# A transformer layer on one core: the ranks of the expert choice through memory instead of TensorE

## The chip, the cores and the metric

The kernel runs on one core of one Trainium2 chip. Its engines are TensorE (PE, with its weight loads PEld), VectorE (DVE), ScalarE (ACT), GpSimd (POOL) and SyncE (SP), which issues nearly all DMAs here. The metric is the device time of one execution in microseconds. Times of three runs and one profiled execution are given.

## What is computed

The input is x of shape (4, 1024, 128), all in fp32. The layer is a causal attention with 16 heads of 8, and then a layer of 8 experts of which each token uses one:

```python
x = x + attention(layernorm(x), Wq, bq, Wk, bk, Wv, bv, Wo, bo)      # causal softmax, 16 heads of 8
h = layernorm(x)
logits = h @ gate_w.T                                                # 8 experts
sel, rw = argmax(logits), sigmoid(max(logits))
for e in range(8):
    xs = h * (rw * (sel == e))[:, None]
    out = out + (xs @ w_up[e].T) * silu(xs @ w_gate[e].T) @ w_down[e].T    # inner size 64
x = x + out
```

## The kernel before, in words

The attention takes the first four fifths of the time: 16 units of 4 heads, each with its scores, exponentials and values. Behind it stand the **expert steps**, STEPS = 8, one for each half (512 tokens) of each of the 4 sequences. Each engine has a program of its own, written by hand in the order in which it runs, and semaphores between them; there is no scheduler.

Step n of the experts handles 512 tokens as 4 tiles of 128. The experts go in PAIRS = 4 pairs of 2 x 64 = 128 inner rows. TensorE computes for each pair a gate product into two banks in turn (`gate`, L1244) and an up product (`up`, L1249), both 128 x 512 in fp32, and each such call shows in the trace as two matmuls. ScalarE takes the silu of the gate (`back`, L808). VectorE multiplies by 1 or 0, depending on whether the token's expert is the one of the row (`choose`, L991), and by the up product (`back`, L997), which gives `hidden`. TensorE multiplies by the down weights (`down`, L1258), first pairs 0 and 1, then 2 and 3. VectorE adds the residual (`finish`, L1003, tile y), and SyncE stores y (`store`, L488).

`choose` must know for every token, along the free dimension and in all partitions, which expert it has. That is the **rank**: `residual(n)` on VectorE computes it with one token per partition, four numbers in each (`rank`, L974), at the end of the work of step n - 2. To get it into all partitions, TensorE multiplies, with each of the four columns broadcast as weights, by the identity (`spread_rank`, L1231) into a PSUM bank, and ScalarE copies the bank into `rank_b` (`copy_rank`, L789). In TensorE's order `spread_rank(n + 1)` stands between the two halves of `down(n)`, ahead of `turn_xs` (L1037), which transposes the scaled input `xs` of step n + 1; ScalarE's copy `copy_xs` (L793) takes that one into `xs_t`. VectorE prepares `xs` with `weigh_rows` (L979, L982).

Further back in the chain of a step stand the projection of the attention (`project3`, L1220) for step n + 2, in the middle of step n, and ahead of it GpSimd's product with the inverse sums (L658), which needs two DMAs: the reload of the attention values and of the inverses (`load_attn`, L459 and L461). SyncE's queue in the expert steps is: reload of step n, store of step n - 3, reload of step n + 1, and so on, each behind a semaphore wait. A wait there holds up all that is behind it. `invert` (L927) on VectorE and `store_inverse` (L454) give the inverses of the last batch early in step 2.

## Time and profile before

| what | us |
|---|---|
| median of 3 runs | 525.75 (525.52 to 526.53) |
| profiled execution | 523.49 |
| its span | 521.8 |
| one expert step (steps 2 to 6) | 12.03 |
| PE busy | 493.5 |
| DVE busy | 441.8 |
| ACT busy | 376.4 |
| POOL busy | 225.7 |

The span is the time between the first and the last instruction that the profiler has; what lies around it belongs to the execution too. Busy times of PE contain overlaps, since matmuls are pipelined. A profile names an instruction by its engine, the line of the kernel, the operation and the tiles out<-in. In a timeline a piece begins at the start of its first instruction, and a bracket behind it tells how long the engine sat idle before it and who released it. In the chain of waits each piece begins where the one before ends. The expert steps begin at 424.12 us of the span, and step 3, from which most rows below are, at 448.41.

### The profile page before, as it was taken

What the parts mean: (1) busy time and instruction counts of PE and PEld (TensorE: products, weight loads), DVE (VectorE), ACT (ScalarE), POOL (GpSimd) and SP (SyncE); (2) the same over time, 40 slices, a digit from 0 to 9 for tenths busy, and PEclk for the clock granted to TensorE, in tenths of its full rate; (3) what the DMA queues carried; (4) which work ended last, traced back from release to release, by engine and by line L of the source; (5) the groups of instructions that cost most, each with busy time, mean ns of one, the idle gap of its engine ahead of it and who ended that gap; (6) DMA issues with size and microseconds to landing.
All of it is one profiled execution on the core that took longest, in us unless ns stands there. A gap on an engine that the chain in (4) does not pass through costs nothing.

```text
span 521.8 us, 12773 instructions
## 1 busy us (share of the span) xinstructions
PE 493.5 (95%) x4797; PEld 218.2 (42%) x4797; DVE 441.8 (85%) x695; ACT 376.4 (72%) x790; POOL 225.7 (43%) x526
## 2 busy tenths in 40 slices
PE   7699799999999999999999999999999899999997
PEld 6565324333332433324333332433333236777764
DVE  6958799999999999999998999999995428888864
ACT  7254698888989888898888989888797872222321
POOL 5397266353453635446363444634344142222210
PEclk9889999999999999999999999999999999999999
DMA  6252023422203232221423202112030212221001
GB/s 176 58 137 62 12 74 80 103 62 76 74 19 96 69 92 63 28 71 30 107 60 78 74 10 68 40 53 69 13 94 19 61 39 67 61 63 62 20 22 40
DMA packets 33550, 32.63 MB, mean 63 GB/s; under 512 B 10448, under 2 KB 26960, under 8 KB 33488
## 3 DMA queue, kind: packets, MB, share of 16 engines
q1 hardware_dynamic: 33376, 31.48, 22.8%
q8 instruction: 38, 0.62, 0.5%
q10 hardware_dynamic: 112, 0.33, 0.2%
q14 instruction: 24, 0.20, 0.1%
HBM read 20.26 MB, written 11.01 MB: 60 GB/s over the span
## 4 chain that ended last, share of the span: by engine, by line
PE 59%; DVE 30%; POOL 3%; ACT 3%; issue 3%; DMA 1%; ACTq 0%; DVEq 0%; POOLq 0%
PE ps L1191 18%; DVE top_p L890 11%; PE ps L1175 10%; PE ps L1136 8%; DVE top_p L885 7%; DVE top_p L887 6%; PE ps L1258 5%; PE ps L1244 5%; PE ps L1249 5%; POOL xn L564 2%; ACT sum_sb L759 2%; PE ps L1220 2%; DVE top L906 2%; PE ps L1144 2%; ACT prob L768 1%
## 5 line engine op out<-in xcount | busy, mean ns | idle before, releaser
L768 ACT ACTIVATE prob<-ps 128x512 f32<-128x512 f32 (+2 forms) x640 | 303.9, 564 | 35.1 <-PE ps L1175 33.6
L645 POOL TENSOR_SCALAR_AFFINE_SELECT prob<-prob 128x256 f32<-128x256 f32 x256 | 99.8, 417 | 181.4 <-ACT prob L768 178.6
L1175 PE MATMUL ps<-q_rows,k_rows 51*128 51x512 bf16 (+3 forms) x768 | 170.8, 328 | 3.3 <-ACT prob L768 1.6
L1191 PE MATMUL ps<-prob,v_all 128*9 128x512 f32 (+3 forms) x1536 | 156.9, 488 | 2.3 <-POOL prob L645 0.7
L885 DVE TENSOR_REDUCE top_p<-ps 128x2 f32<-128x1024 f32 x128 | 150.9, 1220 | 9.6 <-PE ps L1136 8.6
L1136 PE MATMUL ps<-k_rows,q_rows 48*128 48x128 bf16 (+3 forms) x1024 | 113.3, 265 | 7.4 <-DVE top_p L890 4.5
L1175 PEld LDWEIGHTS ps<-q_rows,k_rows 51*128 51x128 bf16 x768 | 53.0, 94 | 148.2 <-ACT prob L768 131.3
L890 DVE TENSOR_REDUCE top_p<-ps 128x8 f32<-128x1024 f32 x64 | 76.6, 1220 | 10.7 <-PE ps L1144 10.2
L887 DVE TENSOR_REDUCE top_p<-ps 128x4 f32<-128x1024 f32 x64 | 75.2, 1215 | 1.8 <-PE ps L1136 1.8
L1136 PEld LDWEIGHTS ps<-k_rows,q_rows 48*128 48x128 bf16 x1024 | 45.4, 94 | 27.2 <-DVE top_p L890 9.0
L1191 PEld LDWEIGHTS ps<-prob,v_all 128*9 128x9 f32 x1536 | 24.3, 88 | 52.2 <-issue 29.5
L808 ACT ACTIVATE prob<-ps 128x512 f32<-128x512 f32 x32 | 19.1, 597 | 32.7 <-PE ps L1244 20.1
L991 DVE SCALAR_TENSOR_TENSOR prob<-rank_b,rank_of,prob 128x512 f32<-128x512 f32 x32 | 23.3, 750 | 16.1 <-ACT prob L808 15.3
L1244 PE MATMUL ps<-xs_t,w_g 128*128 128x512 f32 x64 | 31.6, 596 | 0.0
L1249 PE MATMUL ps<-xs_t,w_u 128*128 128x512 f32 x64 | 31.4, 592 | 0.0
L1258 PE MATMUL ps<-w_d,prob 128*128 128x128 f32 x256 | 31.0, 275 | 0.0
L1258 PEld LDWEIGHTS ps<-w_d,prob 128*128 128x128 f32 x256 | 29.9, 192 | 1.0 <-issue 1.0
L1144 PE MATMUL ps<-shade,pick 64*128 64x256 bf16 (+1 forms) x160 | 29.4, 296 | 0.0
L759 ACT ACTIVATE sum_sb<-ps 128x512 f32<-128x512 f32 x32 | 19.0, 594 | 13.4 <-PE ps L1191 13.4
L663 POOL TENSOR_SCALAR spread<-moments 128x4 f32<-128x4 f32 x8 | 1.6, 195 | 55.4 <-DVE moments L969 55.3
L892 DVE TENSOR_REDUCE top_p<-ps 128x16 f32<-128x1024 f32 x16 | 19.5, 1221 | 6.8 <-PE ps L1144 6.4
L789 ACT ACTIVATE rank_b<-ps 128x512 f32<-128x512 f32 x8 | 4.8, 600 | 27.5 <-PE ps L1231 27.5
(110 smaller groups left out, 451.8 us busy)
## 6 DMA issues: line engine op xcount, KB each, us to landing
split_parts<-part SPq DMA_DIRECT2D x12, 384.0 KB, 4.4
q_rows<-split_parts SPq DMA_DIRECT2D x31, 96.0 KB
k_rows<-split_parts SPq DMA_DIRECT2D x31, 96.0 KB
value_sums<-sum_sb SPq DMA_DIRECT2D x128, 18.0 KB
x_sb<-x SPq DMA_DIRECT2D x8, 256.0 KB, 4.2
qk<-value_sums SPq DMA_DIRECT2D x8, 256.0 KB, 3.6
qk<-inverse_sums SPq DMA_DIRECT2D x8, 256.0 KB, 4.0
out<-y SPq DMA_DIRECT2D x8, 256.0 KB, 2.3
```

The source lines that it names most:

```text
L645: last = g.affine_select(out=quarter, in_=quarter, pattern=[[0, GH], [1, Q]], base=Q * (1 - z), channel_multiplier=-1, compare_op=ALU.is_g ...
L768: a.activation(prob[:, i % NB, g0:g0 + heads, 0:cols], ps[:, load_at(u, n) % 3, 0:heads * cols].rearrange("p (s t) -> p s t", s=heads), AC ...
L885: return v.tensor_reduce(top_p[:, c, place, s:s + 3:2, m], banks, AX.X, ALU.max)
L887: return v.tensor_reduce(top_p[:, c, place, :, m], banks.rearrange("p r (s t) -> p (r s) t", s=2), AX.X, ALU.max)
L890: return v.tensor_reduce(top_p[:, c, place, :, :].rearrange("p g m -> p (g m)"), banks.rearrange("p r (y t) -> p (r y) t", t=P), AX.X, ALU ...
L1136: last = mm(ps[:, first_bank + rg, cols], q_rows[rows, k, c, s, q0:q0 + P], k_rows[rows, k, 0 if width == HALF else c, s, k0:k0 + width], ...
L1144: last = mm(dst, pick[rows, PICK[tile]:PICK[tile] + P], shade[rows, None, :].to_broadcast((64, len(blocks), Q)), start=False, stop=True, s ...
L1175: last = mm(ps[:, l % 3, m * cols:(m + 1) * cols], k_rows[rows, k, j // TPH, s + m, j % TPH * P:(j % TPH + 1) * P], q_rows[rows, k, c, s + ...
L1191: last = mm(ps[32 * g:32 * g + HD + 1, BANK_V, q0:q0 + n], v_all[:, b, j, first_head + g, :], prob[:, i % NB, g, 0:n], start=(j == 0), sto ...
L1244: mm(ps[:, BANK_GATE[pr % 2], :], w_g[:, pr * P:(pr + 1) * P], xs_t[:, h, :], start=True, stop=True).then_inc(gate_mm, 1)
L1249: mm(ps[:, BANK_UP[pr % 2], :], w_u[:, pr * P:(pr + 1) * P], xs_t[:, h, :], start=True, stop=True).then_inc(up_mm, 1)
L1258: last = mm(ps[:, BANK_DOWN, i * P:(i + 1) * P], hidden[:, pr, i * P:(i + 1) * P], w_d[:, pr, :], start=(pr == 0 and i == 0), stop=(pr == ...
```

## The change

From step 2 on, the rank no longer goes over TensorE, a bank and ScalarE. `rank` becomes fp32. SyncE writes its 512 numbers to a small tensor in memory (`ranks`), waits until they have landed, and reads them back as one row repeated into all 128 partitions of `rank_b` (`send_rank`). `choose` waits for that read. Step 1 keeps the old way, with a tile `rank_1` in bf16; TensorE's wait for its copy moves from the first gate product to the up product that uses its bank.

```diff
+    ranks = nc.dram_tensor("ranks", (STEPS, TPH, P), FP32, kind="Internal").ap()
...
-        rank = sb("rank", [P, 2, TPH], BF16)
+        rank_1 = sb("rank_1", [P, TPH], BF16)
+        rank = sb("rank", [P, 2, TPH])
...
+            def send_rank(n):
+                h = (n - 1) % 2
+                sp.wait_ge(rank_set, n)
+                sp.dma_start(ranks[n - 1].rearrange("i (p o) -> p i o", o=1), rank[:, h, :, None],
+                             allow_slow_non_contiguous=True).then_inc(rank_out, 16)
+                sp.wait_ge(rank_out, 16 * (n - 1))
+
+                hold(sp, chosen_set, 4 * (n - 2))
+                sp.dma_start(rank_b[:, h, :], ranks[n - 1:n].rearrange("o i p -> o (i p)").to_broadcast((P, HALF))
+                             ).then_inc(rank_in, 16)
...
             load_sums(BATCH - 1)
+            send_rank(2)
             store(0, 0)
+            send_rank(3)
...
                 reload(n)
                 store(*divmod(n - 4, 2))
-            for n in range(STEPS - 2, STEPS + 1):
+                send_rank(n - 1)
+            store(*divmod(STEPS - 3, 2))
+            send_rank(STEPS)
+            for n in range(STEPS - 1, STEPS + 1):
                 store(*divmod(n - 1, 2))
...
                 if more:
-                    copy_rank(n + 1, 1 - h)
                     copy_xs(n + 1, 1 - h)
...
-                v.tensor_reduce(rank[:, h, :], hit[:, h], AX.X, ALU.max).then_inc(rank_set, 1)
+                v.tensor_reduce(rank[:, h, :] if n > 1 else rank_1[:], hit[:, h], AX.X, ALU.max).then_inc(rank_set, 1)
...
-                dve.wait_ge(rank_b_set, n)
+                if n == 1:
+                    dve.wait_ge(rank_b_set, 1)
+                else:
+                    dve.wait_ge(rank_in, 16 * (n - 1))
...
             def gate(n, n4, h, pr):
                 if pr == 0:
-                    pe.wait_ge(rank_b_set, n)
                     pe.wait_ge(xs_t_set, n)
...
             def up(n4, h, pr):
                 hold(pe, hidden_set, n4 + pr - 1)
+                if (n4, pr) == (0, 1):
+
+                    pe.wait_ge(rank_b_set, 1)
...
                 down(n, n4, (0, 1))
                 if more:
-                    spread_rank(n + 1, 1 - h)
                     turn_xs(n + 1, 1 - h)
                 down(n, n4, (2, 3))
```

On TensorE, from the up products at the end of step 6 to the first gate products of step 7, before:

```order
L1249 MATMUL ps<-xs_t,w_u 128x512 [waits hidden_set] x2
L1220 MATMUL ps<-w_o,rest 128x136 [waits attn_set]
L1220 MATMUL ps<-w_o,rest 128x136 x3
L1258 MATMUL ps<-w_d,prob 128x128 [waits hidden_set,y_set]
L1258 MATMUL ps<-w_d,prob 128x128 x7
L1231 MATMUL ps<-ident_b,rank 128x128 [waits silu_set,rank_set]
L1231 MATMUL ps<-ident_b,rank 128x128 x3
L1037 MATMUL ps<-ident,xs 128x128 [waits xs_set]
L1037 MATMUL ps<-ident,xs 128x128 x3
L1258 MATMUL ps<-w_d,prob 128x128 [waits hidden_set]
L1258 MATMUL ps<-w_d,prob 128x128 x7
L1244 MATMUL ps<-xs_t,w_g 128x512 [waits silu_set,xs_t_set,rank_b_set]
```

And the same place after, where the lines of the file have other numbers (L1271 is up, L1242 the projection, L1280 down, L1059 the turning, L1263 gate):

```order
L1271 MATMUL ps<-xs_t,w_u 128x512 [waits hidden_set] x2
L1242 MATMUL ps<-w_o,rest 128x136 [waits attn_set]
L1242 MATMUL ps<-w_o,rest 128x136 x3
L1280 MATMUL ps<-w_d,prob 128x128 [waits hidden_set,y_set]
L1280 MATMUL ps<-w_d,prob 128x128 x7
L1059 MATMUL ps<-ident,xs 128x128 [waits xs_set]
L1059 MATMUL ps<-ident,xs 128x128 x3
L1280 MATMUL ps<-w_d,prob 128x128 [waits hidden_set]
L1280 MATMUL ps<-w_d,prob 128x128 x7
L1263 MATMUL ps<-xs_t,w_g 128x512 [waits silu_set,xs_t_set]
```

The four matmuls with the ranks as weights are gone, and with them the waits for VectorE's rank and, at the first gate product, for ScalarE's copy.

On SyncE, from the load of the last batch's sums to the stores of steps 1 to 3, before:

```order
L450 DMA inv<-value_sums 128x1x128 [waits sum_out_1,sum_out_0]
L488 DMA out<-y 128x4x128 [waits y_set]
L454 DMA inverse_sums<-inv 128x128 [waits inv_set]
L459 DMA qk<-value_sums 128x1x512 [waits attn_set]
L461 DMA qk<-inverse_sums 128x1x512
L488 DMA out<-y 128x4x128 [waits y_set]
L459 DMA qk<-value_sums 128x1x512 [waits attn_set]
```

And after:

```order
L455 DMA inv<-value_sums 128x1x128 [waits sum_out_1,sum_out_0]
L504 DMA ranks<-rank 128x4x1 [waits rank_set]
L509 DMA rank_b<-ranks 128x512 [waits rank_out]
L493 DMA out<-y 128x4x128 [waits y_set]
L504 DMA ranks<-rank 128x4x1 [waits rank_set]
L509 DMA rank_b<-ranks 128x512 [waits chosen_set,rank_out]
L459 DMA inverse_sums<-inv 128x128 [waits inv_set]
L464 DMA qk<-value_sums 128x1x512 [waits attn_set]
L466 DMA qk<-inverse_sums 128x1x512
L493 DMA out<-y 128x4x128 [waits y_set]
L504 DMA ranks<-rank 128x4x1 [waits rank_set]
L509 DMA rank_b<-ranks 128x512 [waits chosen_set,rank_out]
```

The ranks of step 2 now stand ahead of the first store, those of step 3 behind it and ahead of the inverses' store, and those of step n + 2 behind the store of step n; what stood behind a store now stands behind the landing of a rank write as well.

## Rows read from the trace of the kernel before

**Rows 1.** The page, part 1: engine, busy us, share of span, instructions.

```profile
PE 493.5 (95%) x4797; PEld 218.2 (42%) x4797; DVE 441.8 (85%) x695; ACT 376.4 (72%) x790; POOL 225.7 (43%) x526
```

**Rows 2.** Busy time of each engine in windows: steps 3, 6 and 7.

```profile
core 0: us, PE busy (x) PEld busy (x) DVE busy (x) ACT busy (x) POOL busy (x), PEclk, DMA share, GB/s
...
448.41:460.44 12.03, 12.03 (x66) 8.19 (x65) 9.70 (x28) 3.57 (x7) 2.62 (x5) 1.00 0.24 68
...
484.51:496.54 12.03, 12.03 (x66) 8.19 (x65) 9.69 (x28) 3.58 (x7) 2.62 (x5) 1.00 0.08 22
496.54:507.65 11.11, 11.11 (x58) 7.27 (x57) 7.20 (x14) 3.57 (x7) 0.57 (x2) 1.00 0.09 24
```

**Rows 3.** Chain of waits, 440 to 522 us: start us, us, what.

```profile
by line: PE ps L1258 30.5%; PE ps L1249 28.3%; PE ps L1244 26.2%; PE ps L1220 5.7%; PE ps L1037 3.2%; PE ps L1231 1.6%; DVE y L1003 0.8%; issue 0.0%
...
455.44 0.93 PE ps L1220 x8
...
458.15 0.22 PE ps L1231 x4
458.38 0.44 PE ps L1037 x4
458.82 1.79 PE ps L1258 x16
```

**Rows 4.** Instructions on the tile rank: ns min/median/max, first and last start.

```profile
L1231 PEld LDWEIGHTS ps<-ident_b,rank x32: 96/98/100, 413.3 to 505.3; 128*128 128x128 bf16 x32
```

**Rows 5.** TensorE's timeline in steps 3 and 7: start us, us, instructions.

```profile
453.56 1.88 PE L1249 MATMUL ps<-xs_t,w_u 128*128 128x512 f32 x4
...
505.42 0.61 PE L1037 MATMUL ps<-ident,xs 128*128 128x128 f32 x4
```

**Rows 6.** VectorE's timeline, from the lead-in to step 7.

```profile
416.81 0.19 DVE L974 TENSOR_REDUCE rank<-hit 128x4 bf16<-128x32 f32 x1
...
438.14 1.61 DVE L991 SCALAR_TENSOR_TENSOR prob<-rank_b,rank_of,prob 128x512 f32<-128x512 f32 x2
...
450.17 1.61 DVE L991 SCALAR_TENSOR_TENSOR prob<-rank_b,rank_of,prob 128x512 f32<-128x512 f32 x2 [0.87 <-ACT prob L808]
...
452.90 0.69 DVE L997 TENSOR_TENSOR prob<-ps,prob 128x512 f32<-128x512 f32 x1 [0.52 <-PE ps L1249]
...
453.70 1.12 DVE L982 TENSOR_SCALAR xs<-x_sb,moments,weight 128x128 f32<-128x128 f32 x4
...
456.06 1.28 DVE L997 TENSOR_TENSOR prob<-ps,prob 128x512 f32<-128x512 f32 x2
...
460.64 0.69 DVE L1003 TENSOR_TENSOR y<-ps,x_sb 128x512 f32<-128x512 f32 x1 [0.66 <-PE ps L1258]
...
504.19 1.28 DVE L997 TENSOR_TENSOR prob<-ps,prob 128x512 f32<-128x512 f32 x2
```

**Rows 7.** ScalarE's timeline in step 3.

```profile
458.41 0.60 ACT L789 ACTIVATE rank_b<-ps 128x512 f32<-128x512 f32 x1 [4.05 <-PE ps L1231]
458.91 0.59 ACT L793 ACTIVATE xs_t<-ps 128x512 f32<-128x512 f32 x1
```

**Rows 8.** SyncE's timeline: start of the issue, its us, the DMA.

```profile
427.46 0.52 SPq L450 DMA_DIRECT2D inv<-value_sums  x1
...
438.15 0.35 SPq L454 DMA_DIRECT2D inverse_sums<-inv  x1
...
449.77 0.52 SPq L459 DMA_DIRECT2D qk<-value_sums  x1
```

**Rows 9.** The copies of the tile gate_q: issues and landing.

```profile
L445 SPq DMA_DIRECT2D gate_q<-gate_x x8: 635/640/1368, 211.6 to 216.4; - x8
...
DMA to landing us min/median/max: 2.0/2.3/2.8
```

**Rows 10.** DMA issues: count, KB each, median us to landing.

```profile
out<-y SPq DMA_DIRECT2D x8, 256.0 KB, 2.3
...
b_qk<-bk SPq DMA_DIRECT2D x1, 0.5 KB, 2.6
```

**Rows 11.** The reloads into the tile qk: landing.

```profile
DMA to landing us min/median/max: 3.4/3.8/5.4
```

**Rows 12.** GpSimd's timeline: the product behind the reload of step 5.

```profile
449.01 1.27 POOL L658 TENSOR_TENSOR rest<-qk 128x512 f32<-128x512 f32 x1
```

More of the change, by code:

```diff
@@ L232, in layer_kernel @@
         BANKS_PROJ, BANK_TURN, BANK_GATE, BANK_UP, BANK_DOWN = (5, 6), 7, (0, 1), (2, 4), 3
-        BANK_RANK, FIRST_RANK = BANK_GATE[0], BANK_UP[1]
+        FIRST_RANK = BANK_UP[1]
         def wide(banks):
@@ L315, in layer_kernel @@
         rank_b_set = sem("rank_b_set")
+        rank_out = sem("rank_out")
+        rank_in = sem("rank_in")
         xs_set = sem("xs_set")
@@ L784, in tanh, with copy_rank @@
                 a.activation(weight[:, h, :], scaled[:, h, :], ACT.Tanh).then_inc(tanh_set, 1)
-            def copy_rank(n, h):
-                act.wait_ge(rank_mm, n)
-                hold(act, hidden_set, 4 * (n - 2))
-                a.activation(rank_b[:, h, :], ps[:, BANK_RANK if n > 1 else FIRST_RANK, :], ACT.Copy).then_inc(rank_b_set, 1)
+            def copy_rank():
+                act.wait_ge(rank_mm, 1)
+                a.activation(rank_b[:, 0, :], ps[:, FIRST_RANK, :], ACT.Copy).then_inc(rank_b_set, 1)
             def copy_xs(n, h):
@@ L798, in lead_in @@
                 if n == FRONT["rank"] + 2:
-                    copy_rank(1, 0)
+                    copy_rank()
                 if n == FRONT["turn"] + 2:
@@ L1223, in project3, with spread_rank @@
                     last.then_inc(proj_mm, 1)
-            def spread_rank(n, h):
-                pe.wait_ge(rank_set, n)
-                bank = BANK_RANK if n > 1 else FIRST_RANK
-                hold(pe, silu_set, 4 * (n - 1) - 1)
+            def spread_rank():
+                pe.wait_ge(rank_set, 1)
                 for i in range(TPH):
-                    last = mm(ps[:, bank, i * P:(i + 1) * P], rank[:, h, i:i + 1].to_broadcast((P, P)),
+                    last = mm(ps[:, FIRST_RANK, i * P:(i + 1) * P], rank_1[:, i:i + 1].to_broadcast((P, P)),
                               ident_b[:], start=True, stop=True)
@@ L1272, in lead_in @@
                 if n == FRONT["rank"]:
-                    spread_rank(1, 0)
+                    spread_rank()
                 if n == FRONT["turn"]:
```

## The prediction

> **What bounds the kernel now.** I read the page first. Part 1 gives TensorE as the busiest engine, 95% of the span [rows 1]. But an average doesn't say what a fifth of a microsecond in one stage is worth, so I cut the span by expert step, from the first gate matmul of a step to that of the next [rows 2]. The reader is to see three things there: PE is busy for the whole of every step (12.03 of 12.03 us), at granted clock 1.00, the upper of its two levels; steps 2 to 6 all last 12.03 or 12.04 us; step 7, which has no projection of a later step, lasts 11.11 us. VectorE has 9.7 us of work per step, ScalarE 3.6, GpSimd 2.6. The chain of waits says the same by its pieces: from 440 us on, PE's lines have 95.5% of the time and the last sum on VectorE 0.8%; no other engine stands in it [rows 3]. So in the expert steps every instruction that TensorE gets rid of shortens the kernel, and everything else is free as long as it stays hidden.
>
> The profiled execution took 523.49 us, its span is 521.8, and 1.69 us lie around the span. The median of the three timed runs is 525.75 us, 2.26 above the profiled one. The sum below is made on the span and then taken off the median: nothing in the change touches what lies outside.
>
> **What it removes on TensorE.** Seven times (steps 2 to 8; step 1 keeps its own) the four bf16 matmuls that spread the ranks go. What counts is how far each pushes the next piece back: in the chain the rank piece stands from 458.15 to 458.38 and takes 0.22 us for four [rows 3], 55 ns each. The turning of xs behind it already waits for nothing (xs is ready 3 us earlier: VectorE ends it at 453.70 + 1.12 = 454.82 [rows 6]), so it moves up by the whole 0.22. Seven such pieces: 7 x 0.22 = **1.54 us**.
>
> Does what PE meets next hold it up? From the VectorE rows of step 3 [rows 6]: the last product for the down matmuls (L997) ends at 456.06 + 1.28 = 457.34; the second half of the down matmuls starts at 458.82 by the chain [rows 3], 1.48 behind it. After the removal 1.26 of that is left. The fourth up matmul needs the product that ends at 452.90 + 0.69 = 453.59, starts at 453.56 + 0.86 = 454.42 [rows 5], 0.83 us later, and is not moved relative to it. The tight place is step 7, where no projection stands between: products end at 504.19 + 1.28 = 505.47 [rows 6], and the second half of down starts behind the turning, at 505.42 + 0.44 = 505.86 [rows 3, 5]. Moved up by 0.22 it starts at 505.64, 0.17 us behind the product. If that is too little for the semaphore, step 7 gives back a part of its 0.22. So the sum is 1.54, with 1.32 as its lower end from this.
>
> Its upper end is from the weight loads: each rank matmul has a load of 98 ns [rows 4]. Were PE paced by loads here, the seven pieces would be worth 28 x 0.098 = 2.74 us. I take 0.055, since the chain measures starts of real matmuls, and the load row of a step is 8.2 us busy of 12.03 [rows 2]. The Trainium skill, "TensorE: Matmul & The Clock Gate", section "Back-to-back issue gap", states about 81 ns for each of a sustained stream of load and matmul pairs at 128 columns, beside 56 ns for the isolated gap. By the 81 ns the removal would be worth an estimated 2.27 us; the trace's 0.22 us for four speaks for the smaller number.
>
> **What it removes on ScalarE.** Seven copies of 0.60 us. ScalarE waits 4 us for the rank matmuls before each, and the copy of the turned xs behind it starts at 458.91, when its own matmuls are just done (458.38 + 0.44 = 458.82) [rows 3, 7]. It ends at 459.50, and gate starts at 460.44 [rows 2]. Worth: 0. In the changed kernel both ends move up together, and the slack of 0.94 stays.
>
> **What it adds: the round trip.** SyncE now writes 2 KB of ranks as 512 runs of 4 bytes, waits for the landing, and issues a read of 256 KB that puts the row of 2 KB into every partition. No such DMA is in the trace. For the write the nearest row is the gate_q copies: 64 partitions x 8 tiles = 512 runs of 32 bytes each, landing after 2.0 to 2.8 us, median 2.3; loads of 128 runs of 4 bytes land after 2.6, where they are counted from their issue [rows 9, 10]. For the read it is the reload of inverse_sums, which also repeats rows of 2 KB: both reloads land after 3.4 to 5.4, median 3.8 [rows 11]. I take 2.3 + 3.8 + 0.1 for the wake-up = **6.2 us** (bounds: 2.0 + 2.3 = 4.3, with the landing of a store of 256 KB as the lower end of the read [rows 10], and twice the slowest, 5.4 + 5.4 = 10.8).
>
> When is it due? Ranks of step 2: they are ready at 417.0 [rows 6], but SyncE comes to them behind the load of the sums, issued at 427.46 + 0.52 [rows 8]. So they are sent at 428.0 and land at 434.2; the first use in step 2 is at 438.14 [rows 6], or 0.22 earlier in the changed kernel. Slack 9.9 - 6.2 = 3.7 us. Ranks of step 4: sent behind the store of step 2, at 449.77, where the reload stands now [rows 8]; first use 12.03 us after the 450.17 of step 3, at 462.20. Slack 12.2 - 6.2 = 6.0 us. The ranks of steps 3 and 5 to 8 lie as those of step 4. With 10.8 us the ranks of step 2 alone would be late, by 0.9 us, and PE has the 0.83 us named above between them and a stall. Worth: 0, and 0.1 us lost at the upper bound. A gain from it is excluded, since VectorE's first choose of a step waits for ScalarE's silu, not for the ranks (450.17 [rows 6]).
>
> The Trainium skill, "DMA: Bandwidth & Descriptors", section "Rules for kernel authors", speaks against this write: a last dimension with a stride becomes one descriptor per element, and it advises another layout. The trace has 512-run copies that land in 2.3 us. The page gives no price for such runs; where it is high, the time is that of rival (c).
>
> **What stands behind SyncE's new waits.** SyncE sits out the landing of each write, some 2.4 us, and spends 1.2 us in issues. Behind it are the reloads and the store of the inverses. The inverses of the last batch go out at 438.15 now [rows 8], then at some 441.5; the reload for step 5, right behind it, goes to some 442.5 and lands by 447 if it takes 3.8, by 448.5 if 5.4. GpSimd takes it up at 449.01 [rows 12]. The reload for step 6 moves from 449.77 to some 453.2 and lands by 457 to 459; GpSimd wants it one step after the 449.01, at 461.05. Were it later, GpSimd's product still has from 450.28 to the projection at 455.44, 5 us more [rows 3, 12]. Of the stores of the output, those of steps 1 to 6 leave ahead of the rank that goes with them, and the last two have no new wait ahead of them that ends late: the last store follows the last sum as before. Worth: 0.
>
> VectorE writes ranks in fp32 instead of bf16, 4 numbers per partition at 0.19 us [rows 6]: 0. TensorE's wait for the first rank copy moves from gate to an up matmul of step 1, and that copy ended long before the experts start: 0.
>
> **Sum:** 7 x 0.22 = 1.54 us off TensorE, on the path; 0 for the rest. 525.75 - 1.54 = **524.2 us**, 0.29% faster; the profiled span would be near 520.3.
>
> **Rivals.**
> (a) PE can't use all of it: slack on other engines turns out shorter than I read it, in step 7 first and then in the others (VectorE's chain gate, silu, choose, product is as long as before while PE's step shrinks). Each step that doesn't shorten keeps 0.22. If half of them don't, the gain is 0.8 us: 525.0. For it: 0.17 us in step 7. Against it: 1.26 us in the others.
> (b) The loads pace PE in the rank piece: 525.75 - 2.74 = 523.0. For it: 98 ns per load against 55. Against: the piece's 0.22 us. The skill's 81 ns lies between.
> (c) The round trip is late, and the kernel is **slower**. Ranks of step n+2 are sent behind y of step n, and y of step n+2 comes 11.2 us after that step's first choose (450.17 to 461.33 [rows 6]); so two steps can't be shorter than L + 0.44 + 11.2, L being the round trip. Against 2 x 11.81 = 23.6 this decides from L = 12.0, and each further us costs half a us per step for six steps. At L = 14 that is 6 - 1.54 = 4.5 us slower, 530.2; slower by 0.2% begins near L = 12.9. What could do it: 4-byte writes into memory that cost several times the 2.3 us of the 32-byte ones, since no row shows such a write. Against: the slowest two landings shown add to 10.8.
> (d) The ranks arrive in time, but the transfers behind SyncE's waits don't: a reload that lands 7 us behind the 447 reckoned above holds up the projection at 455.44, since GpSimd's 1.27 us lie between. At some 8.5 us the gain is eaten, 525.7. The slowest landing shown is only 1.6 us above the 3.8 taken.
>
> **How the numbers follow.** Forecast 0.70; (a) 0.10; (b) 0.07; (c) 0.07; (d) 0.06. A measurement of this kernel can tell about 0.2% (1.05 us) from no change. Faster: forecast and (b), 0.77, less 0.05 for a forecast of 1.54 that is measured below 1.05 = 0.72. Same: (a), (d) and those 0.05 = 0.21. Slower: 0.07. Range: from (b) at 523.2 to the gain-eaten cases at 525.7; it leaves out (c) and a few hundredths at the other end.
>
> **What would show it.** Right: steps 2 to 6 of the new trace at 11.81 us and step 7 at 10.89, PE busy throughout; VectorE's first choose of a step still released by ScalarE's silu and not by a DMA; the rank write landing in 2 to 3 us, the read in 3 to 4; SyncE's reloads 3 to 4 us later with GpSimd still released by VectorE's moments. Wrong: choose released by the read of the ranks, or any step with PE idle; a rank write that lands after more than 5 us; a step that still lasts 12.03 without the four matmuls.

## The result

The changed kernel took a median of 537.93 us (535.49 to 539.75, 4 runs) against 525.91 before: a ratio of 1.0214, with a 95% interval of 1.0178 to 1.0250. The forecast was 524.2, faster. Below, one execution of e13 (537.30 us) is left out of its figures, since it lies more than 1.5% above the fastest of its kernel; every other one is counted. The profiled execution took 538.88 us, its span is 537.2. The attention part of that execution is 2.3 us longer than before's (the first expert step starts at 426.45 instead of 424.12); the rest of the difference lies in the expert steps, from their start to the end of the span: 110.75 us instead of 521.80 - 424.12 = 97.68. I use this length below, since it leaves out what the attention part varies by from run to run.

Busy time of each engine in windows, kernel after, one window for each expert step (columns as in [rows 2]):

```profile
core 0: us, PE busy (x) PEld busy (x) DVE busy (x) ACT busy (x) POOL busy (x), PEclk, DMA share, GB/s
426.45:438.48 12.03, 12.03 (x64) 8.00 (x61) 8.82 (x27) 4.85 (x8) 3.01 (x5) 1.00 0.09 13
438.48:454.98 16.50, 13.75 (x63) 8.54 (x61) 10.55 (x29) 3.08 (x6) 3.28 (x6) 0.90 0.23 52
454.98:466.78 11.80, 11.80 (x62) 7.98 (x61) 9.70 (x28) 3.08 (x6) 2.14 (x4) 1.00 0.31 71
466.78:483.95 17.17, 13.69 (x63) 9.52 (x61) 9.60 (x28) 3.08 (x6) 3.47 (x6) 0.90 0.48 106
483.95:495.75 11.80, 11.80 (x62) 7.98 (x61) 9.70 (x28) 3.08 (x6) 1.87 (x3) 1.00 0.10 23
495.75:510.33 14.58, 12.34 (x62) 7.81 (x61) 10.30 (x28) 3.08 (x6) 2.40 (x5) 1.00 0.38 80
510.33:521.21 10.88, 10.88 (x55) 7.06 (x53) 7.35 (x15) 3.08 (x6) 1.18 (x2) 1.00 0.20 40
```

Set beside [rows 2], two kinds of steps are to be seen. Steps 3, 5 and 7 are what was forecast: 11.80, 11.80 and 10.88 us, each 0.23 shorter than before, PE busy throughout. Steps 2, 4 and 6 take 16.50, 17.17 and 14.58, and PE is idle in them. Who waits for what, kernel after, from the first expert step on (us in total, times, longest):

```profile
POOL rest L679 <- DMA qk<-inverse_sums: 19.7, 4, 8.3
...
DVE prob L1013 <- DMA rank_b<-ranks: 14.1, 4, 4.2
```

VectorE's choose (L991 before, L1013 now) was released by ScalarE in step 3 of before [rows 6]; now four of the steps (2, 4, 6 and 8) wait for the read of the ranks, 14.1 us in all. GpSimd waits 19.7 us for reloads, and before it waited for none here. Both come from one DMA, whose landing the DMA issues of after show, beside the neighbours it has (KB each, median us to landing):

```profile
qk<-value_sums SPq DMA_DIRECT2D x8, 256.0 KB, 4.3
qk<-inverse_sums SPq DMA_DIRECT2D x8, 256.0 KB, 5.1
out<-y SPq DMA_DIRECT2D x8, 256.0 KB, 6.5
...
rank_b<-ranks SPq DMA_DIRECT2D x7, 256.0 KB, 4.2
...
ranks<-rank SPq DMA_DIRECT2D x7, 2.0 KB, 10.2
```

The 2 KB of ranks take 10.2 us to land, where I had taken 2.3 from [rows 9]. The store of y, 2.3 us in [rows 10], takes 6.5; the rank write goes out right behind it, and in e12 below, with the same order of DMAs and the write spread in memory, the store takes 2.2. The chain of waits of after shows how this reaches TensorE. In step 2 the ranks themselves are late: write and read take 14.1 us together, and VectorE's choose waits 4.25 us.

```profile
430.36 10.69 DMA ranks<-rank
441.04 0.02 issue
441.06 3.40 DMA rank_b<-ranks
```

In steps 3 and 4 it is what stands behind the write:

```profile
456.33 8.10 DMA ranks<-rank
464.43 0.02 issue
464.45 0.33 SPq L509
464.78 0.04 issue
464.82 1.94 SPq L464
466.76 0.04 issue
466.81 9.10 DMA qk<-inverse_sums
475.91 0.07 issue
475.98 1.27 POOL rest L679
477.25 0.04 issue
477.29 2.18 PE ps L1242 x8
```

SyncE sits 8.1 us on the landing of the write, then issues the reload, which takes 9.1 us instead of 3.8 [rows 11]; the next rank write goes out 1.3 us behind it (at 468.13), and e2 and e3 below show that such a write holds up a reload. GpSimd's product and TensorE's projection come late. And the DMA engines are not busy meanwhile (windows of after, DMA share is the last but one column):

```profile
456.40:458.00 1.60, 1.60 (x6) 0.65 (x5) 1.15 (x2) 0.93 (x3) 0.00 (x0) 1.00 1.02 247
458.00:464.40 6.40, 6.40 (x33) 4.25 (x32) 5.84 (x14) 1.19 (x2) 1.42 (x1) 1.00 0.04 2
```

Soon after 458.0 the DMA engines have done with the store and the write; for 6.4 us they move next to nothing (share 0.04, and 0.00 from 458.50 to 464.00), and only then is the write reported as landed. The first write, issued at 430.36 with no store in front of it, shows it more plainly: the trace's records of its 4-byte packets last 7 to 9 ns each, the last one ends at 431.91, and the landing is at 441.04. The time is not spent in sending 512 runs, but in what comes after.

**Where the 13 us come from.** Step 2: PE idle 2.75 us (16.50 - 13.75), and 1.94 in the up products behind it (3.66 us for four, 1.72 in other steps). About 1.7 of that is the lower clock: behind idle time at the full clock the four take 1.98 (e13 below). Step 4: PE idle 3.48, and the projection takes 2.18 instead of 0.93 [rows 3], the down product behind it 2.41 instead of 1.78; together 5.36, all of the step's 17.17 - 11.80. Some 1.6 of it is the clock, since in step 6 the projection behind idle time takes 1.19 at the full clock. The granted clock of both steps is 0.90 in the mean: behind the idle time it stood at the lower of the two levels (1.2 GHz), 0.51 from 446.5 to 450.0 and 0.50 from 477.3 to 479.4. Step 6: 2.8, with 2.24 us of idle time and the clock at 1.00. The last step, with choose waiting 4.0 us for the ranks, is 2.0 longer than in e1 (15.99 and 13.98). Sum 4.7 + 5.4 + 2.8 + 2.0 = 14.9, less some 1.8 us that the missing matmuls give back (97.68 - 95.90, from e1): 13.1 (110.75 - 97.68).

### The profile page after: what moved, and what is told of

It reads as the page before. It is cut to its first block, busy times and chain, and to the rows that moved or that the text cites. A ratio compares the mean times of both kernels' runs of the same rounds, so it can differ in the third digit from the quotient of the medians.

```text
span 537.2 us, 12717 instructions
## 1 busy us (share of the span) xinstructions
PE 498.9 (93%) x4769; PEld 219.1 (41%) x4769; DVE 442.6 (82%) x695; ACT 372.6 (69%) x783; POOL 225.5 (42%) x526
## 4 chain that ended last, share of the span: by engine, by line
PE 46%; DVE 29%; DMA 13%; POOL 4%; ACT 3%; issue 3%; SPq 1%; ACTq 0%; DVEq 0%; POOLq 0%
PE ps L1213 18%; DVE top_p L909 10%; PE ps L1197 10%; PE ps L1158 8%; DMA ranks<-rank 7%; DVE top_p L904 7%; DVE top_p L906 6%; DMA qk<-inverse_sums 3%; PE ps L1280 3%; POOL xn L585 2%; ACT sum_sb L780 2%; DMA rank_b<-ranks 2%; PE ps L1166 2%; DVE top L925 1%; PE ps L1242 1%
## 5 line engine op out<-in xcount | busy, mean ns | idle before, releaser
L1013 DVE SCALAR_TENSOR_TENSOR prob<-rank_b,rank_of,prob 128x512 f32<-128x512 f32 x32 | 22.8, 748 | 27.2 <-DMA rank_b<-ranks 14.1
L1271 PE MATMUL ps<-xs_t,w_u 128*128 128x512 f32 x64 | 33.4, 625 | 6.0 <-DVE prob L1019 6.0
L1280 PE MATMUL ps<-w_d,prob 128*128 128x128 f32 x256 | 31.7, 279 | 0.0
L1263 PE MATMUL ps<-xs_t,w_g 128*128 128x512 f32 x64 | 31.6, 596 | 0.0
L1280 PEld LDWEIGHTS ps<-w_d,prob 128*128 128x128 f32 x256 | 30.7, 196 | 1.0 <-issue 1.0
L813 ACT ACTIVATE xs_t<-ps 128x512 f32<-128x512 f32 x8 | 4.8, 596 | 36.1 <-PE ps L1059 36.1
L1019 DVE TENSOR_TENSOR prob<-ps,prob 128x512 f32<-128x512 f32 x32 | 20.9, 683 | 1.6 <-PE ps L1271 1.6
```

Source lines behind the costliest of these rows:

```text
L1263: mm(ps[:, BANK_GATE[pr % 2], :], w_g[:, pr * P:(pr + 1) * P], xs_t[:, h, :], start=True, stop=True).then_inc(gate_mm, 1)
L1271: mm(ps[:, BANK_UP[pr % 2], :], w_u[:, pr * P:(pr + 1) * P], xs_t[:, h, :], start=True, stop=True).then_inc(up_mm, 1)
L1280: last = mm(ps[:, BANK_DOWN, i * P:(i + 1) * P], hidden[:, pr, i * P:(i + 1) * P], w_d[:, pr, :], start=(pr == 0 and i == 0), stop=(pr == ...
```

## Experiments

Two theories stood against each other at first. A: all that costs is the landing of the write, and TensorE's 1.54 us are there. B: the read of one row by all partitions crowds the other DMAs.

**e1: without the write.**

```diff
-                sp.dma_start(ranks[n - 1]..., rank[:, h, :, None], ...).then_inc(rank_out, 16)
-                sp.wait_ge(rank_out, 16 * (n - 1))
-                sp.dma_start(rank_b[:, h, :], ranks[n - 1:n]...
+                sp.dma_start(rank_b[:, h, :], x[0:1, 0:TPH, :]...
```

Since nothing waits for the landings in between, the reads count on two semaphores in turn.

> The changed kernel without the write of the ranks: SyncE reads 512 numbers of the input x into rank_b as soon as the rank of the step is computed, and waits for no landing. The ranks of steps 2 to 8 are therefore not the real ones (the choice of experts is left out in effect), the work of all engines is the same. Theory A (the write is what costs, by its landing of 7 to 11 us, and TensorE does give back 0.22 us per step): 524.0 to 524.5 us, expert steps of 11.81 us, reloads landing in 3.4 to 5.4 us as before. Theory B (the read of one row by 128 partitions, 4.2 us instead of the reloads' 3.8, crowds the other DMAs, and would do so without the write): above 526 us, with reloads of inverse_sums landing after more than 6 us.

Measured 524.21 us (10 runs), ratio 0.9974 (0.9953 to 0.9995). The steps last 12.02, 11.81, 11.80, 11.81, 11.80, 11.80 and 10.88 us, the experts' part 95.90. The read lands after 3.7 to 5.3 us and no step waits for it. B falls; the saving on TensorE is as reckoned, 0.23 us per step.

**e2: write kept, nobody waits for it.**

```diff
-                sp.wait_ge(rank_out, 16 * (n - 1))
-                sp.dma_start(rank_b[:, h, :], ranks[n - 1:n]...
+                sp.dma_start(rank_b[:, h, :], x[0:1, 0:TPH, :]...
```

> As the changed kernel, with the write of 512 runs of 4 bytes, but nobody waits for its landing: rank_b is read from the input x at once (so steps 2 to 8 don't use the real ranks), and each step has a rank tile of its own. Theory A1 (only the wait costs: the ranks and what stands in SyncE's queue behind them are late): 524 to 525 us. Theory A2 (the write also holds up the landing of other DMAs that are in flight beside it, as the 9.1 us of the inverse_sums reload at 466.81 and the 6.5 us of the stores in the trace of after suggest): between 525 and 533 us, with reads of rank_b landing after more than 6 us, since they now come right behind the write.

Measured 533.82 us (4 runs), ratio 1.0164 (1.0132 to 1.0197). A1 falls: a loss of 8 us is there without any wait for the write, where the changed kernel lost 12. What is in flight beside it lands late. The chain of waits of this kernel, around steps 2 and 3:

```profile
445.44 18.79 DMA qk<-inverse_sums
464.23 0.07 issue
464.30 1.27 POOL rest L678
465.57 0.04 issue
465.62 2.18 PE ps L1241 x8
```

A reload of 3.8 us takes 18.79 here, between two rank writes (441.68 and 453.83). The reads of rank_b land after 9.2 to 14.3 us, 13.0 in the median.

**e3: the write alone, in the kernel before.** One more DMA per step at the same place, from x_sb, and no other change.

> The kernel before, with one more DMA per expert step and no other change: 512 runs of 4 bytes (from x_sb, after the rank of the step) into a tensor in memory, at the place of the changed kernel's write, and nobody waits for it until the end. It measures the write by itself. Theory A: it lands after 8 to 11 us also without the round trip. Theory A1: the time stays within 1 us of before (525.9). Theory A2: the reload of the inverses and values behind it lands after 8 to 10 us instead of 3.8, which uses up the 7 us of room that a reload has, so 526 to 532 us.

Measured 527.87 us (8 runs, 525.0 to 532.1), ratio 1.0056 (1.0023 to 1.0089). One DMA of 2 KB per step that nobody uses costs 2 to 3 us: the reloads land after up to 16.9 us, step 5 takes 14.20 instead of 12.03, all others what they took. This is A2 at its lower end, with reloads later than the 8 to 10 us expected. The trace has no landing of the write here, so e6 repeats it.

**e4: 128 runs of 16 bytes.**

```diff
-                sp.dma_start(ranks[n - 1].rearrange("i (p o) -> p i o", o=1), rank[:, h, :, None], ...
+                sp.dma_start(ranks[n - 1]... .rearrange("(p i) -> p i", i=TPH), rank[:, h, :])
...
+                by_tile = rank_b[:, h, :] if n == 1 else rank_b[:, h, :].rearrange("p (t i) -> p i t", i=TPH)
-                v.scalar_tensor_tensor(silu[:, pr % 2, :], rank_b[:, h, :], rank_of[:, pr:pr + 1], ...
+                v.scalar_tensor_tensor(gated, by_tile, rank_of[:, pr:pr + 1], ...
```

> The changed kernel with the ranks in memory in the order in which a partition holds them: 128 runs of 16 bytes instead of 512 of 4, the same 2 KB, read back contiguously; VectorE's choose reads rank_b and silu through views with a stride. If the landing time goes with the number of runs (theory N): about a quarter of it, 2.5 to 4 us, the round trip about 7 us, and 524 to 525 us for the kernel, if VectorE's strided choose costs no more than 0.75 us. If it goes with the writes being smaller than a line of memory, with several of them on one line (theory L, 64 bytes or more): 128 writes of 16 bytes still share lines, so 5 to 9 us, and 525 to 531 us.

Measured 527.95 us, ratio 1.0041 (1.0014 to 1.0067). SyncE issues the read 2.5 to 3.7 us behind the write, as theory N had it and not the 5 to 9 of theory L, and choose no longer waits for a DMA. But the condition on VectorE's choose was not met (groups of instructions on VectorE: count, busy us, mean ns, idle before):

```profile
L1015 DVE SCALAR_TENSOR_TENSOR prob<-rank_b,rank_of,prob 128x512 f32<-128x512 f32 x32 | 37.5, 1213 | 13.4 <-ACT prob L827 13.4
```

With a stride of 16 bytes in one input choose takes 1213 ns in the mean instead of 750 (four of the 32, those of step 1, have no stride). VectorE became the bound: steps 3 to 6 take 12.5 to 12.6 us. So the 2 to 3 us above before in this run are VectorE's, not the write's.

**e5: the same, put in order by ScalarE.** Choose is as in the changed kernel.

```diff
+            def turn_rank(n, h):
+                act.wait_ge(rank_in, 16 * (n - 1))
+                hold(act, chosen_set, 4 * (n - 2))
+                a.activation(rank_b[:, h, :].rearrange("p (i t) -> p i t", i=TPH),
+                             rank_in_sb[:, h, :].rearrange("p (t i) -> p i t", i=TPH), ACT.Copy).then_inc(rank_b_set, 1)
...
                     copy_xs(n + 1, 1 - h)
+                    turn_rank(n + 1, 1 - h)
```

> As e4 (128 runs of 16 bytes, each partition's four ranks together), but VectorE's choose reads a contiguous rank_b again: ScalarE, which has room, puts the row that was read into the order of the tiles with one strided copy per step, behind its copy of the turned xs. Theory: in e4 the round trip was in time and only the strided choose (1213 ns instead of 750) was in the way, so this one keeps TensorE busy in every step, steps of 11.81 us, and takes 524.2 us, 0.25% under before. Rival: the strided copy on ScalarE takes so long, or the read lands so late, that ScalarE's silu of the next step is held up, and the time is that of before or more (525.5 to 528).

Measured 524.19 us (12 runs), ratio 0.9983 (0.9962 to 1.0003), which alone can't be told from no change; e16 repeats it. The steps are 11.80 to 11.81 us, the experts' part 95.90 as in e1. The strided copy takes ScalarE 1.13 us. Step 3 of this kernel in the chain of waits, the counterpart of [rows 3]: the rank piece is gone, and all is PE.

```profile
457.06 0.93 PE ps L1246 x8
457.99 1.78 PE ps L1284 x16
459.77 0.44 PE ps L1063 x4
460.21 1.79 PE ps L1284 x16
```

**e6 to e10: what makes the write slow.** The kernel before, with one write per step that nobody waits for; only the place of the 512 runs of 4 bytes in memory differs.

```diff
 e6   ranks (STEPS, TPH, P)       ranks[n - 1].rearrange("i (p o) -> p i o", o=1)
 e7   ranks (STEPS, P, TPH, 2)    ranks[n - 1, :, :, 0:1]
 e8   ranks (STEPS, TPH, P, 16)   ranks[n - 1, :, :, 0:1].rearrange("i p o -> p i o")
 e9   ranks (STEPS, P, TPH)       ranks[n - 1, :, ::-1].rearrange("p (i o) -> p i o", o=1)
 e10  ranks (STEPS, TPH, P, 2)    ranks[n - 1, :, :, 0:1].rearrange("i p o -> p i o")
```

> The kernel before with one write per expert step that nobody waits for: 512 runs of 4 bytes in the layout of the change, tile by tile, so that the 128 partitions of a tile lie side by side in 512 bytes and all 16 DMA engines write into the same 512 bytes. It is the base for the next two. Landing expected as in the changed kernel: 7 to 11 us, and reloads of up to 9 us or more.

> As e6, the same 512 runs of 4 bytes, but partition by partition with 4 bytes left free between two runs: the 8 partitions that one DMA engine serves write into 256 bytes of their own, and engines share nothing smaller than 256 bytes. Theory S (the landing is slow because many engines write parts of the same 64 bytes): 2.5 to 4 us, as e4's 3.3. Theory N (it goes with the number of small runs, wherever they lie): 7 to 11 us as in e6. Theory L (any partial write into a line that another write of the same engine also hits is serialised): 5 to 11 us here too.

> As e6, the same 512 runs of 4 bytes, each alone in 64 bytes of its own. Theory S: 2.5 to 4 us. Theory L: 2.5 to 4 us as well (this and e7 together tell L from S). Theory N: 7 to 11 us.

> As e6 to e8: the kernel before with 512 runs of 4 bytes per step that nobody waits for. Here the layout is partition by partition without gaps, with the four numbers of a partition in reverse order so that each stays a run of its own: 16 runs in every 64 bytes as in e6, but from 4 neighbouring partitions instead of 16. Theory P (what counts is how many writes hit the same 64 bytes): 8 to 9 us, as e6's 8.8. Theory S (what counts is how many partitions, and so how many DMA engines, write into them): 4 to 5.5 us, nearer to e7's 4.4.

> As e9, tile by tile with 4 bytes free between two runs: 8 runs in every 64 bytes as in e7, but from 8 partitions instead of 2. Theory P: 4 to 5 us, as e7's 4.4. Theory S: 5.5 to 9 us, between e7 and e6.

The landing lines of the tile ranks, in the order e6, e7, e8, e9, e10, one kernel each:

```profile
DMA to landing us min/median/max: 7.9/8.8/12.3
```

```profile
DMA to landing us min/median/max: 3.5/4.4/4.6
```

```profile
DMA to landing us min/median/max: 2.3/2.4/2.9
```

```profile
DMA to landing us min/median/max: 6.7/7.6/9.1
```

```profile
DMA to landing us min/median/max: 3.5/4.1/5.3
```

| kernel | runs of 4 bytes in 64 bytes | from partitions | landing, median us |
|---|---|---|---|
| e8 | 1 | 1 | 2.4 |
| e7 | 8 | 2 | 4.4 |
| e10 | 8 | 8 | 4.1 |
| e9 | 16 | 4 | 7.6 |
| e6 | 16 | 16 | 8.8 |

The number of runs is 512 in all five, so theory N, as the number alone, falls with e8. e7's 4.4 lies in the range of neither S (2.5 to 4) nor L (5 to 11). Theory S, that it matters how many partitions write into one place, falls with e10 (4.1, not 5.5 to 9) and e9 (7.6, not 4 to 5.5). Which partitions share a DMA engine no run here shows, so e7's "engines share nothing smaller than 256 bytes" is an assumption; what the table compares is partitions. Theory P holds but for a rest (e9's 7.6 is just under its 8): the landing goes with how densely the small writes lie. In e8, e9 and e7 the records of the 4-byte packets last 7 to 9 ns each, as in the changed kernel, so the layouts differ in what comes behind the packets.

Number or size counts after all where the writes lie densely. e4 and e9 both fill 2 KB partition by partition, e4 in 128 runs of 16 bytes (4 in 64 bytes) and e9 in 512 of 4: at most 2.5 to 3.7 us, from write to read issue, against 7.6. With e8 (1 in 64 bytes, 2.4), e7 and e10 (8, about 4.2) and e6 (16, 8.8) this is one row by the number of writes in 64 bytes. The small stretch of memory is not the cause by itself, since e4's 2 KB are no more than e6's.

The neighbours follow: the slowest reload lands after 15.2 us in e6, 10.8 in e9, 7.7 in e7, 7.0 in e10 and 5.2 in e8 (5.4 before [rows 11]). These kernels had one run each, so their times say little (524.76 to 527.80, in no order of the landings); the experts' part is 97.6 to 98.0 in all of them.

**e11 and e12: the changed kernel with its waits, dense and spread writes.** Both read rank_b from x; e12 alone has the layout of e8.

```diff
-    ranks = nc.dram_tensor("ranks", (STEPS, TPH, P), FP32, kind="Internal").ap()
+    ranks = nc.dram_tensor("ranks", (STEPS, TPH, P, 16), FP32, kind="Internal").ap()
...
-                sp.dma_start(ranks[n - 1].rearrange("i (p o) -> p i o", o=1), rank[:, h, :, None],
+                sp.dma_start(ranks[n - 1, :, :, 0:1].rearrange("i p o -> p i o"), rank[:, h, :, None],
```

> The changed kernel, write and waits as they are, except that the read of rank_b takes 512 numbers of the input x instead of the ranks, so steps 2 to 8 don't use the real ranks. It is the control for e12. Expected: as the changed kernel, 535 to 540 us, and a landing of the write of 8 to 11 us.

> As e11, but the 512 runs of 4 bytes lie each alone in 64 bytes of memory. Number and size of the runs, SyncE's order and all waits are those of the changed kernel; steps 2 to 8 don't use the real ranks. If the whole loss is the landing of writes that share 64 bytes: the write lands after 2.3 to 3 us and the kernel takes 524 to 525 us. If the wait in SyncE's queue, or 512 small runs as such, cost by themselves: above 526 us.

e12: 523.39 us (4 runs, 523.20 to 523.82), ratio 0.9946 (0.9926 to 0.9966); write landed after 2.1 to 3.7 us, steps of 11.80 and 11.81. With the same number of runs, the same order in SyncE's queue and the same waits, the loss is gone when the runs lie apart. Against e11 on the same chip it is the layout alone. e11, though, was a miss: 527.74 us (524.54 to 532.15, 9 runs), ratio 1.0045 (1.0013 to 1.0077), far under the 535 to 540 expected. Its write landed after 8.7 us, its read after 3.6. This profile is of the fastest of the nine (524.54), so it shows less than the usual loss: the experts' part is 98.31 there against e12's 95.94.

**e13 to e16: on one chip, what e11 left open.** e13 is the changed kernel, e14 is e11, e16 is e5. In e15 each rank is sent ahead of its store, here in the loop and likewise for the first and the last:

```diff
                 reload(n)
-                store(*divmod(n - 4, 2))
                 send_rank(n - 1)
+                store(*divmod(n - 4, 2))
```

> The changed kernel once more, on the same chip as e14 to e16. If the loss of 12 us is the kernel's own: 535 to 540 us. If it depends on the chip or on how long the shared writes take there, as e11 suggests, whose write landed after 8.7 us instead of 10.2: the round trip is that landing plus 3.6 to 4.2, and the time follows it, 526 us where it is 12.3 and 538 where it is above 14.5.

> e11 once more (rank_b is read from the input x, the real ranks are written and waited for but not used in steps 2 to 8). If what is read makes no difference, it is within 2 us of e13 on the same chip. If reading back what has just been written is slower than reading x: e13 is longer by half a us per step for each us that its read lands later, and the write's landing is the same in both.

> The changed kernel with each rank sent ahead of the store that it stood behind. The ranks are ready 1.4 us before that store can go, and the store takes 0.4 us to issue, so each round trip begins 1.8 us earlier. By the loop of two steps (round trip + 0.44 + 11.2 us) this is worth half of 1.8 us per step, for six steps about 5 us at most, as long as the round trip decides: 3 to 6 us under e13. If the loss came from SyncE's blocked queue and the late reloads instead: within 1.5 us of e13, since these wait for the same landing.

> e5 once more, beside the changed kernel on one chip: 128 runs of 16 bytes, put in order by ScalarE. Expected 0.2 to 0.4% under before, and expert steps of 11.81 us, whatever e13 does here, since its round trip of 6 to 7 us leaves 5 us of slack.

| kernel | us, median (range) | ratio (95%) | write to read issue, us | read landing |
|---|---|---|---|---|
| e13 changed | 529.24 (528.03 to 535.32) | 1.0076 (1.0040 to 1.0112) | 8.3 to 10.2 | 4.4 |
| e14 reads x | 527.33 (525.30 to 530.80) | 1.0034 (1.0006 to 1.0063) | 7.9 to 10.4 | 3.2 |
| e15 sent first | 529.87 (529.34 to 535.00) | 1.0104 (1.0036 to 1.0171) | 7.4 to 9.6 | 4.5 |
| e16 by token, ScalarE | 523.87 (521.84 to 525.86) | 0.9965 (0.9943 to 0.9986) | 2.0 to 2.9 | 3.6 |

The changed kernel is slower than before here too, but by 0.8% and not by 2.1%, and its own runs reach from 528 to 535. In the first profile the write took 8.1 to 11.4 us, here 8.3 to 10.2.

Where the two profiled executions differ can be read from them: the experts' part is 110.75 us in the first and 100.77 in e13. TensorE's four up products behind the late ranks of step 2, the first line from the changed kernel and the second from e13:

```profile
446.55 3.66 PE L1271 MATMUL ps<-xs_t,w_u 128*128 128x512 f32 x4 [2.75 <-DVE prob L1019]
```

```profile
445.27 1.98 PE L1271 MATMUL ps<-xs_t,w_u 128*128 128x512 f32 x4 [2.00 <-DVE prob L1019]
```

Behind 2.75 us of idle time the clock is at its lower level, behind the 2.00 of e13 it is not (granted 1.00 in every step of e13). With step 4, the clock is some 3.3 of the 10.0 us; the rest is idle time, half of it in step 4, where the reload landed after 9.1 us in the first and after 6.2 at most in e13.

In e11, e13 and e14 the reloads land after 3.4 to 6.2 us, little later than before's 5.4, and GpSimd still waits 12 to 15 us for them. There it is SyncE's queue that is late, and not the landing of the neighbours; and TensorE never waits for GpSimd's product for more than 0.7 us in these three.

The read lands after 4.4 us in e13 and after 3.2 in e14, and e14 is 1.9 us shorter, with intervals that still touch. That just written data come back more slowly can't be concluded from it: in e1, with the reloads right behind it, the read of x took 4.5.

e15 misses the 3 to 6 us; it lies within the 1.5 us of e13 that were expected if SyncE's blocked queue and the late reloads make the loss. The waits of choose for the ranks did shrink, as the lines of e13 and then of e15 show,

```profile
POOL rest L679 <- DMA qk<-inverse_sums: 14.6, 4, 4.3
DVE prob L1013 <- DMA rank_b<-ranks: 13.7, 6, 3.5
```

```profile
POOL rest L679 <- DMA qk<-inverse_sums: 17.0, 4, 6.8
DVE prob L1013 <- DMA rank_b<-ranks: 5.5, 2, 3.7
...
PEld ps L1242 <- POOL rest L679: 3.2, 2, 2.0
```

from 13.7 us to 5.5, but GpSimd now waits 17.0 instead of 14.6 for the reloads, and TensorE waits for GpSimd in two steps. Steps 5 and 8 get shorter by 1.3 and 0.9 us, steps 2, 3 and 4 longer by 1.8, 1.5 and 0.2; in step 2 1.6 of that is the clock again (3.61 us for the four up products, 1.98 in e13). With 4 executions, and one profile of each, this shows that sending the ranks earlier moved the waits and did not shorten the kernel; what each way costs by itself it does not separate.

e16 repeats e5's result beside it: 0.35% under before, steps of 11.80 us. It is the version to keep, about 1.8 us better than the kernel before, and no engine waits for its round trip in the trace. e12, though faster still, is no such version, since it reads x instead of the ranks.

## Why the prediction was wrong, step by step

**TensorE's share was right.** 7 x 0.22 = 1.54 us: in e1, e5, e12 and e16 steps 2 to 6 shorten from 12.03 to 11.80 or 11.81 and step 7 from 11.11 to 10.88, PE busy throughout, and the experts' part from 97.68 to 95.90 to 95.98. The first seven steps together are 1.61 us shorter in e1 (83.53 to 81.92), seven times 0.23; the other 0.17 lie in the last step and were not in the sum. The tight place in step 7 (0.17 us) held. Rival (b), the weight loads at 98 ns, falls: a step would have been 0.39 us shorter. The Trainium skill, "TensorE: Matmul & The Clock Gate", section "Back-to-back issue gap", has some 81 ns for a sustained stream of pairs; that would have been an estimated 0.32 us per step, and the traces do not agree with it for these four.

**The step that failed is the term for the write.** I took 2.3 us from [rows 9], with 5.4 as the slowest landing of any row, and so 6.2 us for the round trip, 10.8 at most. The write took 8.1 to 11.4, and the four round trips that choose waited for took 13.3 to 15.2. The row was the nearest by the number of runs, 512, and that was the wrong property: those copies write 32 bytes each into SBUF tiles, and e6 to e10 show that at one and the same count of 512 the landing goes from 2.4 to 8.8 us with how densely the 4-byte runs lie in memory. Nothing in the trace of before had small writes side by side in memory, and I treated twice the slowest landing of quite other transfers as a bound. It was none: a row of another kind bounds nothing, and the range had to say so. Rival (c) named just this cause, "4-byte writes into memory that cost several times the 2.3 us", at 0.07. The prediction also knew of the other layout and kept the strided one; e5 and e16 are that other layout, and they give the time that was forecast.

**Rival (c) was right in kind and too cheap.** It gave 530.2 at a round trip of 14 us; the profile has those of 13.3 to 15.2, and 538. For steps 5 and 6 its loop was nearly right: 15.2 + 0.44 + 11.2 = 26.9 us, and the two took 26.4. Missing were three things. The ranks of step 2 have 9.9 us and not 12: the wait of 4.25 us there cost 4.7 us at once, though I had the 9.9 in the sum. TensorE's clock fell behind the idle time, some 1.7 us in step 2 and 1.6 in step 4. And the reload of step 4.

**"What stands behind SyncE's new waits: 0" failed as well.** I let the queue stand for 2.4 us; it stood for 8 to 11. And I took the landing of the reloads as unchanged, while beside a dense write DMAs issued before it and behind it land late. e2 shows that by itself: with no wait at all, 533.8 us. Rival (d) had the place (a reload 7 us late) but only SyncE's wait as the cause.

The Trainium skill, "DMA: Bandwidth & Descriptors", section "Specifications", says that transfers under 512 bytes make the DMA read, modify and write. I had not weighed it. As it stands it would not have given the answer either: the 4-byte runs of e8 and e12 are under 512 bytes too and land after 2.1 to 3.7 us. Only the dense ones are slow.

**Settled and open.** Settled: the loss comes from the landing of the dense write (e12 against e11 in time, e8 against e6 in landing), and it reaches TensorE by three ways: late ranks (step 2), SyncE's queue held up behind the landing (the chain of step 4), and neighbours that land late (the same chain, and e2 with no wait in the queue). How the loss divides among them is not separated. Open: what unit of memory the dense writes meet in, and by what mechanism; I compared spacings of 4, 8 and 64 bytes, not the size of a line. e11 and e12 show the layout's share as 4.35 us, in a kernel that reads x; for the full 12 us of the first measurement there is no such pair. Open too is why one and the same kernel ran at 538 us in one place and at 529 in another. The landings of the write differ by about 1 us in the median, and the traces show how that grows into more (idle time, clock, a late reload), but no run separates the chip from chance.

## What to carry to other kernels

A small write must be priced by how its runs lie at the destination too, and not only by bytes or by the number of runs: put together in a partition what one partition holds, and turn it over later on an engine with room. Before a wait goes into a queue, ask what its landing does to the DMAs already in flight, and not only what stands behind it. And when no row shows a transfer, measure it by itself in the kernel as it stands, unwaited, before building on it; one run of e6 would have said 8.8 us. Where the sum says that a late DMA costs its own lateness, add what the idle time costs at the lower clock, if the trace has rows for it.

## What the runs showed of the hardware

- 512 writes of 4 bytes, side by side in memory, landed after 7.6 to 8.8 us in the median where nobody waited for them (e9, e6) and 10.2 in the changed kernel, 8 in 64 bytes after 4.1 to 4.4, each alone in 64 bytes after 2.4. 128 writes of 16 bytes, side by side, were through after 2.0 to 3.7 us (e4, e5, e16). The packets of the dense write were sent within 2 us of its issue; the rest passed with a DMA share of 0.04 or less.
- While such a write was under way, DMAs beside it landed late: a store 6.5 us instead of 2.3, a reload up to 18.8 instead of 3.8. The store had been issued first.
- TensorE's granted clock stood at 0.50 to 0.51 behind 2.75 us of idle time, and four 128x512 products in fp32 took 3.66 us; behind 2.00 us in e13 it stayed at 1.00, and they took 1.98.
- VectorE's scalar_tensor_tensor of 128x512 in fp32 took 1213 ns in the mean with a stride of 16 bytes in one input, and 750 without; ScalarE's copy with the same stride 1.13 us instead of 0.60.
